# Depthwise stage: residual loads moved to GpSimd, cells numbered by columns, one store for each unit

## The reference

```python
def _L3_conv_ref(x, A_kernel, B_kernel, gate_A_kernel, gate_B_kernel, W_out, b_out, T):
    ...
    gate_A = jax.nn.sigmoid(ifft_real(gA_f[None] * x_f))     # 7x7 depthwise convolutions,
    gate_B = jax.nn.sigmoid(ifft_real(gB_f[None] * x_f))     # written as products of spectra
    a_spatial = ifft_real(jnp.broadcast_to(A_f[None], (B, H, W, C)))
    b_spatial = ifft_real(B_f[None] * x_f)
    a_t = a_spatial * gate_A
    b_t = b_spatial * gate_B
    ...  # T equal steps of a scan in log space
    h_final = jnp.exp(log_h[-1])
    return h_final @ W_out + b_out

x = x + _L3_conv_ref(_gn(x), L3_conv_A_kernel, ..., L3_conv_b_out, 8)
```

## Time and profile before

| | us |
|---|---|
| Runs of the kernel, median of 3 | 4744.89 |
| Lowest and highest of them | 4726.04, 12713.48 |
| The profiled execution, device time | 4727.85 |
| Its span, from the first to the last instruction | 4726.0 |
| Depthwise stage in it, from its first transfer | 3935.74 to 4726.0 |

### The profile page before, as it was taken

One profiled execution on the slowest core, in us unless ns is written; L12 is line 12 of the kernel. 1 busy time (PEld: TensorE's weight loads), 2 busy tenths in 40 slices (PEclk: granted clock), 3 DMA queues, 4 the chain that ended last, 5 costly groups with the idle time before them and its releaser, 6 DMA issues. The chain is left out here.

```text
span 4726.0 us, 106613 instructions
## 1 busy us (share of the span) xinstructions
PE 4350.1 (92%) x34470; PEld 3290.9 (70%) x34470; DVE 3399.5 (72%) x10051; ACT 2866.0 (61%) x7966; POOL 2070.0 (44%) x1786
## 2 busy tenths in 40 slices
PE   6999999999999999766999989999739997999995
PEld 5777777777777777525677767777424446999995
DVE  7888888888888888632666656666328994666665
ACT  0888888888888888212433333333317882666664
POOL 0777777777777777102233323333006660222222
PEclk8999999999999999978999989999869998999997
DMA  7222222222222222795222222222656887999994
GB/s 314 66 77 77 77 77 76 76 77 77 77 78 76 75 76 77 270 388 182 92 71 73 72 88 67 72 72 69 256 196 226 293 282 260 268 287 293 294 292 116
DMA packets 754788, 712.95 MB, mean 151 GB/s; under 512 B 60693, under 2 KB 635412, under 8 KB 745687
## 3 DMA queue, kind: packets, MB, share of 16 engines
q1 hardware_dynamic: 735723, 672.74, 46.1%
q10 hardware_dynamic: 14717, 20.01, 1.2%
q0 software_dynamic: 3808, 13.47, 0.8%
HBM read 506.70 MB, written 199.29 MB: 149 GB/s over the span
## 5 line engine op out<-in xcount | busy, mean ns | idle before, releaser
L308 POOL TENSOR_TENSOR at_bias<-at_tri,at_mask 128x1024 f32<-128x1024 f32 x512 | 1203.7, 2370 | 115.6 <-DMA at_mask<-in_L_conv_mask_bias_dram 110.7
L430 ACT ACTIVATE at_probs<-at_neg_s,at_neg_max 128x256 f32<-128x256 f32 x2048 | 1012.4, 504 | 0.2 <-DVE at_neg_max L474 0.2
L474 DVE CUSTOM_DVE_ANT_0 at_neg_s<-at_p_s,at_bias 128x256 f32<-128x256 f32 x2048 | 761.3, 419 | 18.4 <-PE at_p_s L350 3.7
L974 ACT ACTIVATE ml_h<-ml_p_turns,l_b 128x512 f32<-128x512 f32 x384 | 263.8, 687 | 609.1 <-PE ml_p_turns L933 609.1
L361 PE MATMUL at_p_t<-all_ident,at_probs 128*128 128x128 f32 x4096 | 614.3, 273 | 1.1 <-DVE at_probs_t L482 0.6
L942 PEld LDWEIGHTS ml_p<-l_w1s,ml_h 128*128 128x128 f32 x4096 | 471.9, 192 | 52.7 <-issue 52.7
L361 PEld LDWEIGHTS at_p_t<-all_ident,at_probs 128*128 128x128 f32 x4096 | 487.3, 141 | 28.5 <-ACT at_probs L430 2.5
L933 PE MATMUL ml_p_turns<-ml_h,l_w 128*128 128x512 f32 x1024 | 487.0, 599 | 2.3 <-DVE ml_h L1007 2.3
L942 PE MATMUL ml_p<-l_w1s,ml_h 128*128 128x128 f32 x4096 | 484.6, 277 | 0.8 <-issue 0.8
L1075 POOL TENSOR_TENSOR ml_x2t<-ml_z,ml_xb 128x512 f32<-128x512 f32 x128 | 163.5, 1277 | 678.2 <-DVE ml_z L1041 678.2
L2002 POOL TENSOR_TENSOR dw_room<-dw_room,all_b_plain 128x512 f32<-128x512 f32 x128 | 173.6, 1356 | 600.2 <-DMA dw_room<-x3t 600.2
(11 more groups left out here) (229 smaller groups left out, 9194.1 us busy)
## 6 DMA issues: line engine op xcount, KB each, us to landing
dw_xw<-planes SPq DMA_DIRECT2D x128, 528.0 KB, 4.8
sp_xs<-x SPq DMA_DIRECT2D x128, 512.0 KB, 8.9
dw_wts<-patch_w SPq DMA_DIRECT2D x128, 512.0 KB, 6.1
planes<-pw_plane SPq DMA_DIRECT2D x128, 264.0 KB, 3.1
in_xs<-in_x_dram SPq DMA_DIRECT2D x32, 1024.0 KB, 7.7
at_xs<-in_x_dram SPq DMA_DIRECT2D x256, 128.0 KB, 2.3
at_kvs<-in_L_conv_kv_x_dram SPq DMA_DIRECT2D x256, 128.0 KB, 2.5
at_mask<-in_L_conv_mask_bias_dram SPq DMA_DIRECT2D x256, 128.0 KB, 3.2
```

Of the source, the lines that this page charges most:

```text
L308: pool.tensor_tensor(bias[:, n % 2, part], tri[:, part], mask[:, n % 4].unsqueeze(1).broadcast_to((128, 4, COLS)), ALU.add).then_inc(maske ...
L430: e = act.activation(probs[:, h, qh, :], neg_s[:, n % 2, h, qh, :], ACT.Exp, bias=neg_max[:, n % 2, i:i + 1], scale=-1.0, accum_out=sums[: ...
L474: t = dve.tensor_tensor_reduce(neg_s[:, n % 2, h, qh, :], p_s[h][:, qh, :], bias[:, n % 2, i, :], -1.0, 3.0e38, ALU.add, ALU.min, neg_max[ ...
L974: act.activation(h1[:, b, :], bank_of(hidden_use(t, b))[:, :], ACT.Relu, bias=b0[:, b:b + 1]).then_inc(relu_act, 1)
```

## The change

Four things are changed, all in the depthwise stage but one line in the stage that prepares its weights.

- The residual loads are issued by GpSimd. Its queue first issues the loads of units 0 to 2, and then, for each unit `w`, the four loads of unit `w` + 3 and the bias addition of unit `w`.
- The places in a patch are numbered along its columns, so that the four places of a projection lie above one another, and `hid` is laid out with four places inside (`[.., SPOTS // 4, PX, 4]`). A partition now stands for patch a and row y (4 a + y), and holds the four columns d side by side.
- A unit's result is therefore stored by one transfer with runs of 2 KB on both sides, where there were four with runs of 512 B in the output.
- To bring the values into this order, the turns write their 128 columns into PSUM in runs of four elements (16 B), 64 B apart, and the softplus writes `hid` in two instructions of 256 elements with runs of 16, where one instruction of 512 elements wrote single elements 128 B apart.

```diff
-                    oy, ox = divmod(spot + i, PATCH)
+                    ox, oy = divmod(spot + i, PATCH)
...
-        hid = m.sb("hid", [128, 2, SPOTS, PX])
+        hid = m.sb("hid", [128, 2, SPOTS // 4, PX, 4])
...
-        p_turn = [m.ps(f"p_turn{i}", [128, PATCH, 2 * SPOTS]) for i in range(2)]
+        p_turn = [m.ps(f"p_turn{i}", [128, 2, 2, SPOTS // 4, 4, 4]) for i in range(2)]
...
-            def load_residual(w):
-                r, x, y = w // 4, w // 2 % 2, w % 2 * 4
-                if w >= 4:
-                    sp.wait_ge(added, w - 3)
-                cells = x3t[r // 2, r % 2 * 64:r % 2 * 64 + 64, x:x + PX].rearrange("(y d) a c -> d a y c", d=PATCH)
-                for d in range(4):
-                    sp.dma_start(xr[d * PX:(d + 1) * PX, w % 4], cells[(1 - x) * SHIFT + d][:, y:y + 4]).then_inc(r_loaded[w % 4], 16)
-
             def store(w):
                 r, x, y = w // 4, w // 2 % 2 * 4, w % 2 * 4
                 sp.wait_ge(added, w + 1)
-                for d in range(4):
-                    sp.dma_start(out[0, r * PATCH + y:r * PATCH + y + 4].rearrange("y (a d) c -> d a y c", d=PATCH)[x + d],
-                                 outs[d * PX:(d + 1) * PX, w % 4]).then_inc(stored[w % 4], 16)
+                cells = out[0, r * PATCH + y:r * PATCH + y + 4].rearrange("y (a d) c -> a y d c", d=PATCH)
+                sp.dma_start(cells[:, :, x:x + 4].rearrange("a y d c -> a y (d c)"),
+                             outs[:, w % 4].rearrange("p d c -> p (d c)")).then_inc(stored[w % 4], 16)
...
-                if 0 <= u - 6 < total:
-                    load_residual(u - 6)
...
-                    mm = pe.transpose(p_turn[u % 2][:, i, :], cells, ident[:, :])
+                    places = p_turn[u % 2][:, i // 4, :, :, i % 4].rearrange("p f s y -> p (f s) y")
+                    mm = pe.transpose(places, cells, ident[:, :])
...
-                    mm = pe.matmul(p_out[w % 2][:, i, :], hid[:, r % 2, spot:spot + 4].rearrange("p s a -> p (s a)"),
+                    mm = pe.matmul(p_out[w % 2][:, i, :], hid[:, r % 2, (x + i) * 2 + y].rearrange("p a y -> p (a y)"),
...
+            def load_residual(w):
+                r, x, y = w // 4, w // 2 % 2, w % 2 * 4
+                if w >= 4:
+                    pool.wait_ge(added, w - 3)
+                cells = x3t[r // 2, r % 2 * 64:r % 2 * 64 + 64, x:x + PX].rearrange("(y d) a c -> d a y c", d=PATCH)
+                for d in range(4):
+                    pool.dma_start(xr[:, w % 4, d], cells[(1 - x) * SHIFT + d][:, y:y + 4]).then_inc(r_loaded[w % 4], 16)
+
+            pool.wait_ge(og_conv_ready, 1)
+            for w in range(3):
+                load_residual(w)
             for w in range(total):
+                if w + 3 < total:
+                    load_residual(w + 3)
                 pool.wait_ge(r_loaded[w % 4], 64 * (w // 4 + 1))
                 pool.tensor_tensor(xr[:, w % 4], xr[:, w % 4], b_plain.unsqueeze(1).broadcast_to((128, 4, CH)),
                                    ALU.add).then_inc(biased, 1)
...
-                dve.scalar_tensor_tensor(out=hid[:, r % 2, :, x:x + PATCH].rearrange("p s a -> p a s"), in0=bt[:, u % 3],
-                                         scalar=0.0, in1=soft[:, u % 2], op0=ALU.max, op1=ALU.add).then_inc(hid_made, 1)
+                for half in range(2):
+                    part, at = slice(half * BANK // 2, (half + 1) * BANK // 2), x + half * 4
+                    done = dve.scalar_tensor_tensor(out=hid[:, r % 2, :, at:at + 4].rearrange("p s a y -> p s (a y)"),
+                                                    in0=bt[:, u % 3, part].rearrange("p (s n) -> p s n", n=16), scalar=0.0,
+                                                    in1=soft[:, u % 2, part].rearrange("p (s n) -> p s n", n=16),
+                                                    op0=ALU.max, op1=ALU.add)
+                done.then_inc(hid_made, 1)
```

More of the change, by code:

```diff
@@ L1699, in depthwise_layer @@
         f_shift = m.sb("f_shift", [128, 2])
-        hid = m.sb("hid", [128, 2, SPOTS, PX])
+        hid = m.sb("hid", [128, 2, SPOTS // 4, PX, 4])
         room = m.sb("room", [128, 15, BANK])
-        gate, bt, soft = (room[:, a:z].rearrange("p n (a s) -> p n a s", s=SPOTS) for a, z in ((0, 2), (2, 5), (5, 7)))
+        gate, bt, soft = (room[:, a:z] for a, z in ((0, 2), (2, 5), (5, 7)))
         xr, outs = (room[:, a:z].rearrange("p n (a c) -> p n a c", c=CH) for a, z in ((7, 11), (11, 15)))
         p_conv = [m.ps(f"p_conv{i}", [128, 4, BLOCK_PY * PX]) for i in range(2)]
-        p_turn = [m.ps(f"p_turn{i}", [128, PATCH, 2 * SPOTS]) for i in range(2)]
+        p_turn = [m.ps(f"p_turn{i}", [128, 2, 2, SPOTS // 4, 4, 4]) for i in range(2)]
+        by_patch = [t[:, :, :, :, :, :].rearrange("p h f s a y -> p h f (s a y)") for t in p_turn]
+        og_turn = by_patch[0].rearrange("p h f n -> p (h f n)")[:, 0:2 * CH].rearrange("p (a n) -> p a n", a=2)
         p_out = [m.ps(f"p_out{i}", [128, 4, CH]) for i in range(2)]
@@ L1718, in depthwise_layer @@
         og_final = m.sb("og_final", [KTAPS, CH])
-        og_room = hid[:, :, :, :].rearrange("p r s a -> p (r s a)")
+        og_room = hid[:, :, :, :, :].rearrange("p r s a y -> p (r s a y)")
         og_taken = 0
@@ L1807, in _ @@
                     sp.wait_ge(og_final_ready, 1)
-                    sp.wait_ge(stored[0], 64)
-                    sp.wait_ge(stored[2], 64)
+                    sp.wait_ge(stored[0], 16)
+                    sp.wait_ge(stored[2], 16)
                     store_origin(HALO, 0, SIDE - HALO)
             for s in range(4):
-                sp.wait_ge(stored[s], 64 * (total // 4))
+                sp.wait_ge(stored[s], 16 * (total // 4))
             store_origin(0, ROWS - HALO, HALO)
@@ L1841, in turn @@
                     cells = raw[:, patch, :] if u // units % 2 else raw[:, :, patch]
-                    mm = pe.transpose(p_turn[u % 2][:, i, :], cells, ident[:, :])
+                    places = p_turn[u % 2][:, i // 4, :, :, i % 4].rearrange("p f s y -> p (f s) y")
+                    mm = pe.transpose(places, cells, ident[:, :])
                 mm.then_inc(turned, 1)
             def project(w):
-                r, x, y = w // 4, w // 2 % 2 * 4, w % 2 * 4
+                r, x, y = w // 4, w // 2 % 2 * 4, w % 2
                 pe.wait_ge(hid_made, 4 * r + 4)
@@ L1850, in project @@
                 for i in range(4):
-                    spot = (y + i) * PATCH + x
-                    mm = pe.matmul(p_out[w % 2][:, i, :], hid[:, r % 2, spot:spot + 4].rearrange("p s a -> p (s a)"),
+                    mm = pe.matmul(p_out[w % 2][:, i, :], hid[:, r % 2, (x + i) * 2 + y].rearrange("p a y -> p (a y)"),
                                    w_plain, start=True, stop=True)
@@ L1858, in turn_origin @@
                 for i in range(2):
-                    mm = pe.transpose(p_turn[0][:, i, :], og_xs[:, i, :], ident[:, :])
+                    mm = pe.transpose(og_turn[:, i, :], og_xs[:, i, :], ident[:, :])
                 mm.then_inc(og_turned, 1)
@@ L1912, in gate_first @@
                     act.wait_ge(bt_made, u - 1)
-                act.activation(gate[:, u % 2], p_turn[u % 2][:, :, SPOTS:2 * SPOTS], ACT.Exp,
+                act.activation(gate[:, u % 2].rearrange("p (h n) -> p h n", h=2), by_patch[u % 2][:, :, 1], ACT.Exp,
                                bias=f_shift[:, 1:2], scale=nscale[:, :]).then_inc(gate_step, 1)
@@ L2019, in gated @@
                     dve.wait_ge(hid_made, u - 2)
-                dve.scalar_tensor_tensor(out=bt[:, u % 3], in0=p_turn[u % 2][:, :, 0:SPOTS], scalar=f_shift[:, 0:1],
-                                         in1=gate[:, u % 2], op0=ALU.add, op1=ALU.mult).then_inc(bt_made, 1)
+                dve.scalar_tensor_tensor(out=bt[:, u % 3].rearrange("p (h n) -> p h n", h=2), in0=by_patch[u % 2][:, :, 0],
+                                         scalar=f_shift[:, 0:1], in1=gate[:, u % 2].rearrange("p (h n) -> p h n", h=2),
+                                         op0=ALU.add, op1=ALU.mult).then_inc(bt_made, 1)
             def magnitude(u):
@@ L2041, in residual @@
                 if w >= 4:
-                    dve.wait_ge(stored[w % 4], 64 * (w // 4))
+                    dve.wait_ge(stored[w % 4], 16 * (w // 4))
                 dve.tensor_tensor(outs[:, w % 4], p_out[w % 2][:, :, :], xr[:, w % 4], ALU.add).then_inc(added, 1)
@@ L2056, in origin_window @@
                     chained(dve.tensor_copy(og_win[:, :, first:first + k],
-                                            p_turn[0][:, part, base:base + span * k].rearrange("p (y d) -> p y d", d=k)))
+                                            og_turn[:, part, base:base + span * k].rearrange("p (y d) -> p y d", d=k)))
                 chained(dve.tensor_reduce(og_sum, og_kern[:, 1, :], mybir.AxisListType.X, ALU.add))
```

## The result

The change takes 1.006 times the time of before, interval 1.0039 to 1.0082: some 28 us more (4754.24 us against 4726.04, medians of five runs each, for before the three of the table ahead and two more), within 2%. The profiled execution took 4758.21 us, 30.36 more than that of before. The forecast was +5.4 us and 4733; the time lies inside the range, but the loss is five times the sum. That the range holds it is luck: it reached up to 4785 for slower issues and slower turns, and neither came.

What follows compares the result with a forecast made beforehand. TensorE was taken to bound the middle, and a chain through several engines the tail. Losses of 5 us (tail) and 4.3 (drain) less 3.9 gained (end) gave +5.4 on 4727.85, so 4733 us; range 4712 to 4785.

Steps and rivals of the forecast that it cites:

- softplus term: VectorE's softplus: two halves of 0.42 us, 0.85 together, 0.18 less than now; hidden in middle and tail, so zero.
- the round: GpSimd's four issues and bias, then the residual, with handovers: 4.54 us a unit, 5.23 with a collision; hidden in the middle.
- first rival: Whole stage: GpSimd's queue becomes the bound, from 0.64 us an issue with the collision; about 4795 or 4857 us; chance 0.10.
- second rival: TensorE's turns get slower by short runs in PSUM: 0.30 us a unit, about 4767 us, or doubled, 4844; chance 0.08.
- The tail: Residual 104 to 120: 5 us lost, taken between 0 and 9.3, from bias and magnitude holding each other up.
- the other chain: In the tail, projection and turn through sigmoid, gated, magnitude and residual to the next projection but one: stays 4.65 us a unit.
- third rival: The tail gets shorter, with projection and turns at full clock there: 4726 us, or 4719 with faster issues; chance 0.08.
- The drain: Residual 120 to 127: 22.8 us where it took 18.5, so 4.3 us lost.
- The end: Last residual to corner store, one store issue: 3.9 us after that residual began instead of 7.76, so 3.9 gained.
- The noise: Measurement of the whole kernel: tells about 2% (95 us) from no change.

Runs made afterwards that it cites:

- loads on GpSimd alone: The kernel before with only the residual loads moved to GpSimd, its layout and four stores kept; 1.0053 times the time of before.
- bias in the middle: The change with GpSimd issuing two of the four loads, then adding the next unit's bias, then issuing the other two; 1.0025 times the time of before.
- loads on SP: The change with its new layout and single store, but the residual loads issued by SP as before; 0.9982 times the time of before.
- bias ahead: The change with GpSimd, after the loads of unit w + 3, adding the bias of unit w + 1 instead of w; 1.0046 times the time of before.

## Why the prediction was wrong where it was

**The step that failed** is the softplus term, "Both are hidden: ... 1.19 us before the convolution that could wait for it", with "In the middle both are under 5.33, so the round stays hidden there". The prediction saw that bias and magnitude hold each other up and that the bias would come at a fixed 2.45 us behind the residual. It let the bias meet only the magnitude, though the earlier trace rows show the softplus of before at 2.127 too, and it compared the round with TensorE's unit, where the copy's slack of 1.19 was the limit to compare with. In its place the runs show the bias holding 39 of 110 softplus pairs in the middle, and the copy and the convolution behind them late: 17.9 us where nothing was put down. The price of one hold-up then follows from rows that were at hand. Softplus before: 1.06 us, its copy 1.19 ahead of the convolution:

```profile
4303.99 1.06 DVE L2035 SCALAR_TENSOR_TENSOR dw_hid<-dw_room 128x512 f32<-128x512 f32 x1 [1.77 <-ACT dw_room L1931]
```

In four units the convolution began this much (last column, us) after the 0.87 of its turns:

| | softplus | over 1.06 | less 1.19 | plus 0.15 handover | plus 0.08 for two halves | measured |
|---|---|---|---|---|---|---|
| the change | 2.49 | 1.43 | 0.24 | 0.39 | 0.47 | 0.47 |
| loads on GpSimd alone | 2.92 | 1.86 | 0.67 | 0.82 | (one) | 0.82 |
| bias in the middle | 2.27 | 1.21 | 0.02 | 0.17 | 0.25 | 0.25 |
| loads on SP | 1.84 | 0.78 | under 0 | under 0 | -0.18 | 0 |

The handover is the change's copy end, 4305.96, to the convolution at 4306.11; the 0.08 is what its copy ends later behind two halves (0.60 against 0.52 behind one). They were taken from the first row and hold in the other three. They hold in all units of the change too: 36 convolutions of its middle come late, each behind a softplus of 2.43 us or more, by the softplus's length less 2.02 us (1.06 + 1.19 - 0.15 - 0.08) where the turns take 0.87, and less 2.32 where they take 1.17, which leaves the copy 0.30 more slack (all 36 to 0.02 us). Counted from turn to turn, 37 units are longer than their counterparts before, by 17.85 us together, which is the loss of the middle. In 35 of them the convolution is late; in two (1.24 and 1.38 longer) it is the first turn of a block that waits for a copy behind a held softplus. The 60 magnitudes of the middle that were held cost nothing: no convolution is late but behind a held softplus.

**GpSimd's queue (first rival)** decides from 0.64 us for an issue. At 0.564 it did not bound the middle, and "bias ahead" shows that the loss stays without the round. The experiments with the bias out of the softplus's way show that the hold-up is the whole of it.

**Turns (second rival)**: nothing, as taken. The rule of the Trainium skill ("PSUM — Partial Sum Buffer", section "Specifications (TRN2)") that any non-contiguous pattern slows matmuls significantly is not borne out for runs of 16 B in fp32: 272/307/421 ns in both kernels, and 0.87 and 1.17 us for eight from start to start.

**The tail**: +5 taken from 0 to 9.3, measured +8.3; inside the bounds, nearer the upper one: 5.17 us a unit against 4.54 and 5.23. The distances of its residuals are 4.54 us where nothing is held, 4.93 with a held magnitude and some 6.06 with a held softplus, so here too the softplus was left out. That the bounds hold is partly luck: a held magnitude cost 0.39 us, not the 0.69 of the sum (six of the sixteen units), and a held softplus, which the sum did not have, 1.5 (five units). That the other chain stays at 4.65 was wrong the other way: where the bias keeps out of the way or comes loose from the residual, it goes to 4.1 to 4.3 us a unit (66.2 to 68.3 in four kernels). **The third rival** named such a shortening, but by the clock, and that was granted at 0.71 to 0.79 in these four (4625 to 4690 us; 0.76 before).

**The drain**: +4.3 forecast, +4.3 measured, the round as forecast, though its issues took 2.18 instead of 2.31 and the rest 2.37 instead of 2.23. **The end**: -3.9 forecast, -4.6 measured, from the residual's end to the corner store 3.17 - 0.69 = 2.48 us, where 3.2 was assumed. **The noise**: that a measurement tells only about 95 us from no change was wrong; the interval is some 10 us to either side, so the 28 us are clear of it.

**Left open**: whether one softplus instruction in the new order, or one load for a unit, would help; neither was tried. How much of the 4.5 us between "loads on GpSimd alone" and the change is due to the halves and how much to another phase was not separated. Nor was the shorter tail of those four kernels: of before's 74.4 us five held magnitudes account for some 4, and what the rest is no run shows.

## What to carry to other kernels

Where an operation moves in time, list every instruction on the neighbouring engine that it can now meet, and compare each one's longest row with the slack of what stands *behind* it, not with the period of the bounding engine. An engine's queue that is tied to an event by a wait meets the same neighbour again and again (39 of 110 units here), where a loose one mostly passes it by (8 of 110 before); swapping two steps in that queue (here the bias before the issues) can take the whole loss of the middle away. Time the parts of a change apart: this one is a gain of 0.2% and a loss of 0.8% together.

## What was not expected of the hardware

The hold-up begins before the bias row does. The timeline of the change has a softplus half that began at 4319.77 us, 0.50 us ahead of its bias row; alone, at 0.425, it would have ended 0.07 us ahead of it, and yet it was held:

```profile
4319.43 2.47 DVE L2044 SCALAR_TENSOR_TENSOR dw_hid<-dw_room 128x256 f32<-128x256 f32 x2 [1.61 <-ACT dw_room L1923]
...
4320.27 1.34 POOL L2008 TENSOR_TENSOR dw_room<-dw_room,all_b_plain 128x512 f32<-128x512 f32 x1
...
4319.77 2.13 DVE L2044 SCALAR_TENSOR_TENSOR dw_hid<-dw_room 128x256 f32<-128x256 f32 x1
```

The first row is the pair, the last its second half alone. The pair ended 0.29 us behind the bias. If it went on when the bias row ended, the second half had run about 0.425 - 0.29 = 0.13 us before it was stopped, 0.37 us ahead of the row. That makes a hold of 0.37 + 1.34 = 1.7 us, the 2.47 - 0.76 that the pair lost. It is no single case: of the 44 halves that were held in the change, 42 began more than 0.43 us ahead of their bias row, at most 0.78, and all 44 ended 0.29 to 0.31 us behind its end; all 67 held magnitudes ended 0.56 or 0.57 behind it. The Trainium skill ("Perfetto Trace Analysis", section "GPSIMD Engine Instruction") says that the reported start of a GpSimd instruction that reads a tensor is its first read, some way behind the start of its execution; the row fits that, but no run here shows what GpSimd does in these 0.37 us.
